# One attention and expert layer on one core: the store of the next input's rows moves from slot 53 to slot 87, and the last two weight rounds of each body move with it

## What is computed

```python
h = _L0_tok_ref(x, L0_tok_W, L0_tok_b)          # three shifted rows of 256 -> 256, 8 x 744 tokens
h = h + _L0_attn_ref(_layernorm(h, axis=-1), ...)   # causal attention, 16 heads of 16
h = h + _L0_ffn_ref(_layernorm(h, axis=-1), ...)    # top 2 of 4 experts, 256 -> 1024 -> 256, gelu
```

## Time and profile before

| what | value |
|---|---|
| median of three runs | 1807.99 us (1801.91 to 1815.75) |
| profiled execution | 1800.63 us |
| its span | 1798.9 us |
| mean granted TensorE clock | 0.921 |
| busy share of PE, DVE, POOL, ACT | 85%, 61%, 46%, 39% |
| bodies (about) | 129 to 1100 us |
| experts (about) | 1160 us to the end |

### The profile page before, as it was taken

One profiled execution on the slowest core, in us unless ns is written; L12 is line 12 of the kernel. 1 busy time (PEld: TensorE's weight loads), 2 busy tenths in 40 slices (PEclk: granted clock), 3 DMA queues, 4 the chain that ended last, 5 costly groups with the idle time before them and its releaser, 6 DMA issues.

```text
span 1798.9 us, 33109 instructions
## 1 busy us (share of the span) xinstructions
PE 1530.9 (85%) x10648; PEld 1195.0 (66%) x10648; DVE 1096.3 (61%) x3458; ACT 706.6 (39%) x1463; POOL 835.0 (46%) x912
## 2 busy tenths in 40 slices
PE   2669898897997997988978873399999999999997
PEld 2626565474564564744745421399999999999997
DVE  1356678777677687687776732255555555555554
ACT  0104544544534544445445441033333333333332
POOL 4313434645635636446455252424454445454545
PEclk9759999998898998989989876699999999999999
DMA  2251544645535536436436383645545554645451
GB/s 87 68 127 48 154 106 112 180 113 146 144 95 150 143 95 173 123 109 182 111 110 160 97 224 111 182 148 173 192 160 197 169 194 154 207 159 185 169 190 50
DMA packets 166971, 256.23 MB, mean 142 GB/s; under 512 B 30484, under 2 KB 97998, under 8 KB 166800
## 3 DMA queue, kind: packets, MB, share of 16 engines
q1 hardware_dynamic: 108816, 166.66, 32.1%
q10 hardware_dynamic: 34368, 50.33, 8.9%
q0 software_dynamic: 23616, 37.12, 6.9%
HBM read 173.92 MB, written 75.29 MB: 139 GB/s over the span
## 4 chain that ended last, share of the span: by engine, by line
PE 52%; DVE 12%; DMA 12%; issue 11%; SPq 6%; POOL 3%; ACT 3%; ACTq 0%; DVEq 0%; POOLq 0%
PE yb L1388 15%; PE l1b L1375 14%; PE pab L1099 6%; PE pvb L1199 5%; PE stb L1176 4%; PE mxb L1159 4%; DMA qk_s<-parts 4%; DVE unused L903 4%; DMA qst<-negp 4%; SPq L575 2%; SPq L543 2%; DMA qst<-qk_s 2%; SPq L559 1%; PE rb L1346 1%; DMA spare<-spare 1%
## 5 line engine op out<-in xcount | busy, mean ns | idle before, releaser
L764 ACT ACTIVATE prob<-stb 124x496 f32<-124x496 f32 (+2 forms) x832 | 397.8, 504 | 408.4 <-PE stb L1176 394.5
L1159 PE MATMUL mxb<-kst,qst 96*124 96x372 bf16 (+4 forms) x1024 | 319.4, 344 | 95.2 <-DVE mxp L903 48.1
L903 DVE CUSTOM_DVE_ANT_0 unused<-mxb,mask_row 124x372 bf16<-124x372 f32 (+4 forms) x768 | 351.8, 483 | 68.2 <-PE mxb L1159 65.0
L1388 PE MATMUL yb<-w2p,hp 128*128 x2448 | 339.3, 284 | 9.9 <-DVE yo L1330 9.9
L1176 PE MATMUL stb<-qst,kst 99*124 99x372 bf16 (+4 forms) x1024 | 313.0, 339 | 33.0 <-DMA qst<-negp 16.0
L1375 PE MATMUL l1b<-x2T,w1s 128*128 128x384 f32 x1632 | 336.2, 341 | 1.2 <-DVE x2T L1289 1.2
L1388 PEld LDWEIGHTS yb<-w2p,hp 128*128 128x128 f32 x2448 | 323.6, 189 | 20.3 <-issue 20.3
L1259 ACT ACTIVATE hf<-l1b,b1c 128x384 f32<-128x384 f32 x272 | 158.2, 582 | 340.0 <-PE l1b L1375 336.9
L1375 PEld LDWEIGHTS l1b<-x2T,w1s 128*128 128x128 f32 x1632 | 275.1, 189 | 1.6 <-DVE x2T L1289 1.6
L1159 PEld LDWEIGHTS mxb<-kst,qst 96*124 96x124 bf16 x1024 | 140.8, 145 | 185.3 <-DVE mxp L903 90.8
L1316 DVE CAST hp<-hf 128x384 fp32r<-128x384 f32 x272 | 99.8, 367 | 242.5 <-ACT hf L1259 235.7
(11 more groups left out here) (158 smaller groups left out, 1499.8 us busy)
## 6 DMA issues: line engine op xcount, KB each, us to landing
w1s<-ws SPq DMA_DIRECT2D x34, 2048.0 KB, 8.5
qk_s<-parts SPq DMA_DIRECT2D x64, 279.0 KB, 5.8
xg<-xs SPq DMA_DIRECT2D x34, 396.0 KB
kst<-qk_s SPq DMA_DIRECT2D x32, 279.0 KB, 3.7
qst<-qk_s SPq DMA_DIRECT2D x32, 279.0 KB, 5.3
wraw<-in_w_all ACTq DMA_DIRECT2D x32, 256.0 KB, 6.1
ws<-whi ACTq DMA_DIRECT2D x32, 256.0 KB
ws<-wlo ACTq DMA_DIRECT2D x32, 256.0 KB
```

The lines of the kernel that those rows point to most:

```text
L764: act.activation(dst, src, ACT.Exp, scale=DH ** -0.5).then_inc(exp_done, 1)
L903: done = dve.tensor_tensor_reduce(out=unused[:, n % 2, e * w:(e + 1) * w], in0=src, in1=mask_row[:, T - w:T], scale=1.0, scalar=-3.0e38, o ...
L1159: done = nc.tensor.matmul(out, qst[g % NG][0:ROWS, h + e, TT * i:TT * i + TT], kst[g % NG][0:ROWS, h + e, k0:k0 + w], start=True, stop=True)
L1388: done = nc.tensor.matmul(yb[i][:, 0:D], hp[x][:, n % HPB, 128 * i:128 * i + 128], w2p[w][:, bass.ds(owners[t], 1), m, :], start=(m == 0 a ...
```

## The change

The store of the next input's rows, `h1_store`, moves from slot 53 to slot 87. Weight round 2 has its load, split and store at slots 44, 52 and 71 and not at 47, 57 and 62; round 3 at 78, 84 and 98 and not at 67, 76 and 98. Nothing is added or removed.

```diff
@@ -156,7 +156,7 @@
     put(73, "recip", 0)
     put(75, "spread_out", 0)
     put(79, "spread_in", 0)
-    for n, (load, split, store) in enumerate(((2, 10, 13), (19, 26, 29), (47, 57, 62), (67, 76, 98))):
+    for n, (load, split, store) in enumerate(((2, 10, 13), (19, 26, 29), (44, 52, 71), (78, 84, 98))):
         put(load, "wload", n)
         put(split, "wsplit", n)
         put(store, "wstore", n)
@@ -174,7 +174,7 @@
             put(s, "turn", n)
         for p, s in enumerate((35, 36, 37)):
             put(s, "bias", p)
-        put(53, "h1_store", 0)
+        put(87, "h1_store", 0)
         for n in range(4):
             put(38 + 3 * n, "qk", n)
             put(59 + 3 * n, "qk", n + 4)
```

## The result

The changed kernel takes 1862.92 us (median of 4 runs, 1854.69 to 1865.58), the kernel before 1808.1 us (median of 4, 1801.91 to 1815.75). The ratio is 1.0293, 95% interval 1.0242 to 1.0344: slower, outside the range of 1780 to 1828. The profiled execution after took 1865.58 us, its span is 1863.8 us against 1798.9, at a mean granted clock of 0.907 against 0.921.

The account below looks back on a forecast made before the run. The prediction took TensorE (PE) to bound the kernel, so only waits where PE stands counted. Its terms summed as 1800.6 - 26.4 + 14 + 11 + 3 = 1802.2 us, stated as 1803, range 1780 to 1828.

Parts of the forecast that it names:

- Term 1: Bodies 0 to 6: the mx pass's wait for the stack goes, with some low-clock stretches: -26.4 us, between -15 and -39.
- Term 2: Slot 97: the negated maxima land late under the moved row store, 2 us in each of 7 bodies: +14 us.
- Term 3: Last body: round 3's load lands late behind the row load, so POOL's split and masks wait: +11 us (0 to +14).
- Term 4: The rest: weight store at 71 and split at 84 cost 0.4 us a body, slot 44's load nothing: +3 us.
- the slower one: Rival at slot 97: row store outlives 611 by 4 us or more, the maxima pay in full: 1827 us, chance 0.15.
- all four: The forecast's cases: gain given back (chance 0.50), little given back (0.25), maxima pay in full (0.15), stack stays late (0.10).

Follow-up runs that it names:

- experiment 4: Kernel before with the row store moved to slot 87 and round 3's weight store at slot 85: 1829.24 us, ratio 1.0130.
- experiment 5: As experiment 4, with the fold of group 2 at slot 98, behind the maxima, not at 86: 1819.38 us, 1.0070 to the kernel before.
- experiment 9: Changed kernel with all three 124-partition transfers (row store, finished-rows store, row load) issued as 112 + 12 partitions: 1795.58 us, 0.9945 to the kernel before.
- experiment 3: Changed kernel with round 2's load back at slot 47: 1844.85 us, ratio 1.0206 to the kernel before.
- experiment 11: Changed kernel with all three 124-partition transfers cut in two and round 3's split at slot 90, not 84: 1777.66 us, 0.9838 to the kernel before.
- experiment 6: Changed kernel with only the row store issued in two pieces, 112 and 12 partitions: 1826.81 us, ratio 1.0107 to the kernel before.
- experiment 10: Kernel before with only the row store moved to slot 87, in two pieces, weight rounds at their old slots: 1784.03 us, ratio 0.9878.

## Why the prediction was wrong, step by step

- **Term 1 (-26.4)** was right in kind and too large. The seven waits, 21.2 us, are gone, and slots 66 to 78 are 16.8 us shorter. Not all of a wait comes back: bodies 1, 2 and 5 waited 5.9 us together and gained 1.7. The low clock did go: in the 6 us behind the wait it was 0.51 to 0.77 in four of the seven bodies, and in the changed kernel the 6 us from slot 67 have 1.00 in all seven. What this gave back is inside the 16.8 us and cannot be told apart.
- **Term 2 (+14, bounds 0 to 31)** is one of the two steps that failed. It held the landing of the maxima alone, as an overlap of data. In the changed kernel slots 97 to 104 lose 26.4 us, inside the bounds but nearly twice the term; with the store moved by itself 40.0, above my bound. I had counted how long a small transfer takes to land under the store, but not that its issue, and each issue ahead of it, is held, on ACT's queue too. Of PE's waits in these slots of the changed kernel 11.2 us end with the maxima and 13.9 with an exponential. The fold of slot 86 stands in SP's order between the row store and the maxima. It was in the code, and I named the fold only as traffic. Experiments 4 and 5 put 14.6 us of 40.6 on its place. The sign was in my own rows: behind the store of slot 42 the three maxima took 3.44 us to issue, at slot 97 2.40.
- **Term 3 (+11)** was right: POOL's cast of round 3 in the last body waits 13.97 us for its load, and slots 87 to 97 there lose 10.8. With the row load cut (experiment 9, changed kernel) the wait is 3.03 us. The row after, in the timeline of POOL:

```profile
1135.32 0.61 POOL L699 CAST whi<-wraw 128x512 fp32r<-128x512 f32 x1 [13.97 <-DMA wraw<-in_w_all]
```

- **Term 4 (+3, bounds 0 to 10)** is the other, and the larger miss: 27.4 us, outside its bounds. It failed first by the sentence that round 2's load at slot 44 costs nothing. Its landing does not change, as I said; its issue does, 4.5 to 4.9 us a body, by which slots 42 to 47 lose 8.9 us in all and slots 47 to 66 another 6.5, which experiment 3 gives back by moving that load alone. The other miss is the load of round 3 at slot 78, six slots ahead of its split: the loads of the kernel before land in 3.1 to 8.3 us and a slot there is 0.7 us long. The prediction looked at what stands behind the split and took 0.4 us a body; it is 12.0 us over slots 87 to 97 (experiment 11).
- The numbers add up as -16.8 + 26.4 + 10.8 + 27.4 = 47.8 of 62.8 us. The rest is spread: 8.0 us in slots 0 to 42 of the last body, 3.6 in slots 0 to 42 of the others, 3.1 in slots 78 to 87. Of the 8.0, 3.7 lie in its slots 0 to 10, at a granted clock of 0.64 where before it was 1.00, so a part of the price of a late start is paid in the next body. For the rest no cause is shown: slots 0 to 42 of bodies 0 to 6, where nothing was moved, differ by -5.6 to +9.5 us between the runs.
- The rivals: the slower one had the right place, and its price for it (31 us, and 8 for the clock) lies above the 26.4 measured. It came out at 1827 because it lacked the 27.4 us of term 4, as all four did. Its condition, the store living to 17 us after its issue, cannot be checked: the traces have no landing time for this store.
- The range failed because no case had a price for an issue. Even the four terms at their worst bounds (-15, +31, +14, +10) make 1841, past the 1828 that was stated and still 25 us short of the profiled 1865.58. A bound for an operation behind a slow transfer needs the issue in it.

## What to carry to other kernels

Count the partitions of every large DMA: 124 rows in one piece had 22.1% of the engines for an estimated 12 us (755.6 KB at the 67 GB/s of the earlier trace rows), where 112 + 12 had 99.4%, at the price of one more issue of 0.5 to 0.7 us. A DMA's issue belongs to the time of the engine that issues it, so look for compute and for urgent small transfers behind a slow one on both queues before you move it. And a move that takes a transfer out of one deadline puts it in front of the next: here every body has four such deadlines, 26 slots apart.

## What the runs showed of the hardware

- The issue of a DMA shortly behind a transfer that occupies a quarter of the engines is held: 4.5 to 4.9 us for an issue 1.5 us behind it (bodies 1 to 6 of the changed kernel), 0.3 to 0.6 us for one 6 us behind it (the kernel before). At 7.6 to 12.5 us behind the row store of slot 87 it took 0.3 to 4.7 us. In the last body of experiment 6 one issue, behind the row load, took 12.24 us. What it waits for inside was not measured.
- This crosses the queues. The four DMAs of the fold on SP's queue took 5.0 to 9.4 us to issue behind a store on ACT's queue in the changed kernel, 2.5 to 10.0 in experiment 4, 2.5 to 3.3 in the kernel before, and 2.5 to 5.4 behind the cut store (experiments 6 and 10). Why it crosses was not tried.
- ScalarE starts no exponential while its own issue is held (idle 4.66 us at slot 98, 4.40 at slot 44). TensorE runs two more steps, since the program has two `stb` banks, and then waits: 35.2 us in the changed kernel against 12.2.
- A transfer cut in two helps or not by how the pieces divide: 112 + 12 had 99.4% of the 16 engines and gave 0.9852, 116 + 8 had 21.2% and gave 1.0004.
